# A two-layer attention and expert kernel: the low part of one norm chunk moves from VectorE to GpSimd, with a new order of calls in the first block

## The chip, the core and the metric

The kernel runs on one core of one Trainium2 chip. Its time is the device time of one execution in microseconds; the figure given is the median of several. The engines are TensorE (PE in the profile, its weight loads PEld), VectorE (DVE), ScalarE (ACT), GpSimd (POOL) and SyncE (SP), which here only issues transfers. Each runs its own list of instructions in order and waits on semaphores that the others raise.

## What is computed

The input x is 2 sequences of 1024 rows of 256 values, all float32. Cut to what matters:

```
x  = norm(x + x + softmax(causal(q k^T / 16)) v o_proj)       # q, k, v from norm(x)*gamma+beta, one head of width 256
h  = x + attention16(norm(x)*ln1_w+ln1_b)                     # 16 heads of width 128, rotary positions, causal
x  = norm(x + h + experts(norm(h)*ln2_w+ln2_b))               # 4 experts of width 256, the best 2 of each row mixed
```

(norm has no weights unless they are written behind it; the residual of each layer is added twice, since the layer adds it too.)

## The kernel before

**Split products.** TensorE multiplies in a rounded float32 form. To keep the precision, each operand x is held as a high part (x rounded, written by ScalarE) and a low part (x minus the high part, written by VectorE or GpSimd), and `product` (L438) issues three products: high by high, high by low and low by high. So nearly every tile goes PSUM, then ScalarE for the high part, then VectorE or GpSimd for the low part, and only then TensorE uses it.

**Units.** The attention work is 34 units: unit 0 and 1 are the two sequences in the first layer, units 2 to 33 the 16 heads of the second layer for both. A unit has the calls `project_q` (x = 0 to 3: query and key parts of the two 512-column chunks), `project_v` (4 groups), `scores(u, i)` for the eight 128-row tiles, the row maximum on VectorE (`row_max`), the exponent on ScalarE (`exponent`), `transposes(u, i)` of the probabilities into ps_t, their high part (`high_p`) and low part (`low_p`), and the product with the values (`first_outputs` in units 0 and 1, `outputs` and `out_project` later), which VectorE adds to `acc` (`accumulate`).

**The norms.** For a chunk c of 512 rows of a norm job: `ln_stats` (VectorE: statistics, L1576 to L1588), `ln_power` (GpSimd: the power -0.5, L2181), `ln_apply` (VectorE: four tensor_scalar on 128x256, L1636, or L1626 where x1 is written in place) or `ln_rows` (ScalarE), `ln_transpose` (TensorE, L487), `ln_affine` (ScalarE: weight and bias, once to `hf` in full and once rounded to `hT_hi`), and the low part hT_lo = hf - hT_hi. That last step is done by GpSimd in `ln_low` (L2207) for jobs 1 and up, and for job 0, chunk 1, by VectorE in `split_first` (L1643). Chunk 0 of job 0 is done in two halves by functions of its own (`half_stats`, `half_apply`, `half_transpose`, `half_affine`, `half_split`).

**What sets the order.** Nothing is scheduled at run time. For each engine the function `start` lists the calls of the first block by hand, up to unit 3; then `head(u)` repeats one fixed order for units 3 to 30, and `ends` lists the rest. The first block takes the first 140 us or so of the trace. Buffers are few: ps_m has two banks handed out in turn (`take_bank`, L414: a call waits until the user two before it has been emptied), ps_t has two banks, the rows of a norm chunk one buffer `rows`, and `hf` one. During the start TensorE also multiplies zeros (`warm`, L448), which are calls without use for the result.

Of the kernel before, what the change touches and what calls it, by code (L numbers as in the profile page):

```python
# [7 lines left out]
F32 = mybir.dt.float32  # L8
# [14 lines left out]
CH = 512  # L23
# [81 lines left out]
def build(nc, A):  # L105

    with ExitStack() as ctx:
# [6 lines left out]
        def event(name, order, step=1):  # L114
            return Event(sem(name), list(order), step)
# [94 lines left out]
        later = [key for key in ln_tiles if key[0] >= 1]  # L210
# [38 lines left out]
        hT_lo_dve = event("hT_lo_dve", ln_tiles[:4])  # L249
# [82 lines left out]
        def hT_event(job):  # L332
            return hT_lo_dve if job == 0 else hT_lo_pool
# [77 lines left out]
        def _(pe):  # L411
# [78 lines left out]
            def await_hT(job, c):  # L490
                ready = hT_event(job)
                pe.wait_ge(ready.sem, ready.at(job, c, KD - 1))
# [18 lines left out]
            def project_q(u, x):  # L511
# [181 lines left out]
            def start():  # L693
# [5 lines left out]
                warm(3)  # L699
                half_transpose(0)  # L700
                warm(4)
# [21 lines left out]
                transposes(0, 3)  # L723
                scores(0, 5)
                first_outputs(0, 0, 0)
# [11 lines left out]
                first_outputs(0, 1, 0)  # L737
                project_v(1, 0)
                project_q(1, 2)
                scores(1, 0)  # L740
                scores(1, 1)
                scores(1, 2)
                transposes(0, 7)
                project_q(1, 3)
                first_outputs(0, 1, 1)
                transposes(1, 0)
                scores(1, 3)
                transposes(1, 1)
                project_v(1, 1)
                project_v(1, 2)  # L750
                scores(1, 4)
                first_outputs(1, 0, 0)
                transposes(1, 2)
                transposes(1, 3)
# [15 lines left out]
                first_outputs(1, 1, 0)  # L770
                scores(2, 0)
                transposes(1, 7)
                scores(2, 1)
                project_q(2, 3)
                project_v(2, 2)
                scores(2, 2)
                transposes(2, 0)
                scores(2, 3)
                first_outputs(1, 1, 1)
                project_q(3, 0)  # L780
                transposes(2, 1)
                transposes(2, 2)
                scores(2, 4)
# [181 lines left out]
        def _(act):  # L965
# [36 lines left out]
            def ln_affine(job, c):  # L1002
                m, b = LN_VECTORS[job], job % 2
                for k in range(KD):
                    act.wait_ge(ln_mm.sem, ln_mm.at(job, c, k))
                    n = ln_f.place[job, c, k] - KD
                    if n >= 0:
                        before = ln_tiles[n]
                        ready = hT_event(before[0])
# [4 lines left out]
                    if not job:  # L1014
                        act.activation(hT_hi[:, b, k, c * CH:(c + 1) * CH], src, ACT.Identity, bias=ln_b[:, m, k:k + 1],
                                       scale=ln_w[:, m, k:k + 1])
# [163 lines left out]
            def start():  # L1180
# [16 lines left out]
                high_p(0, 1)  # L1197
                high_first(0, 3)
                exponent(0, 3)
                high_p(0, 2)  # L1200
                high_qk_weights(0, 0)
                high_values(0, 2)
                high_p(0, 3)
                high_values(0, 3)
                exponent(0, 4)
                double(0, 1)
                exponent(0, 5)
                high_p(0, 4)
                ln_affine(1, 0)
                double(1, 0)  # L1210
# [3 lines left out]
                high_first(1, 0)  # L1214
                high_p(0, 6)
                exponent(0, 7)
                high_first(1, 1)
                high_first(1, 2)
                high_values(1, 0)
                exponent(1, 0)  # L1220
                high_p(0, 7)
                high_first(1, 3)
                ln_rows(2, 0)
                exponent(1, 1)
                exponent(1, 2)
                high_p(1, 0)
                high_p(1, 1)
                high_values(1, 1)
                exponent(1, 3)
                high_values(1, 2)  # L1230
                exponent(1, 4)
                high_p(1, 2)
                high_p(1, 3)
                ln_affine(2, 0)
                ln_rows(2, 1)
                high_o_weights(0, 0)
                exponent(1, 5)
                high_values(1, 3)
                add_bias(2, 0)
                high_v_weights(0)  # L1240
                high_p(1, 4)
                ln_affine(2, 1)
                add_bias(2, 1)
                add_bias(2, 2)
                exponent(1, 6)
# [4 lines left out]
                high_values(2, 1)  # L1250
                high_p(1, 6)
                exponent(1, 7)
                high_qk_weights(0, 1)
                double(1, 1)
                high_p(1, 7)
                exponent(2, 0)
                add_bias(2, 3)
                high_p(2, 0)
# [3 lines left out]
                high_qk(2, 3)  # L1262
                exponent(2, 1)
                exponent(2, 2)
                add_bias(3, 0)
                exponent(2, 3)
                high_p(2, 1)
                high_p(2, 2)
                high_values(2, 3)
# [3 lines left out]
                high_qk(3, 0)  # L1273
# [3 lines left out]
                ln_affine(3, 0)  # L1277
                ln_rows(3, 1)
# [11 lines left out]
                exponent(3, 1)  # L1290
                high_qk(3, 2)
                high_qk(3, 3)
                high_o_weights(0, 1)
                exponent(3, 2)
                high_values(3, 1)
# [210 lines left out]
        def _(dve):  # L1506
# [1158 lines left out]
```

## Time and profile before

| | |
|---|---|
| median of 3 executions | 1120.58 us (1119.83 to 1121.37) |
| the profiled execution, its own time | 1120.56 us |
| its span, first to last instruction | 1118.7 us |
| TensorE busy | 1108.5 us, 99% |
| VectorE, ScalarE, GpSimd busy | 74%, 66%, 57% |
| mean granted TensorE clock | 0.997 |

The span leaves out 1.86 us of the profiled execution's time. Busy shares are those of the whole span; what an engine waited for is in the rows on waits. In a timeline row the duration of a TensorE instruction overlaps the next one, so the pace is read from one start to the next; a float32 product (transposes, `warm`) is recorded as two entries where the records are complete.

### The profile page before, as it was taken

To read this page: it belongs to the slowest core of one execution; us is meant where nothing else is said; L and a number is where in the kernel's file an instruction comes from. 1 tells how busy PE (TensorE), PEld (TensorE's weight loads), DVE (VectorE), ACT (ScalarE), POOL (GpSimd) and SP (SyncE) were. 2 spreads that over 40 slices of the span, in tenths; PEclk is the share of its full clock that TensorE was granted. 3 is DMA by queue.
4 is the path that set the end of the run, shared out by engine and by line. 5 is a ranking of instruction groups with operands and counts; after the bars stand their busy time and mean duration, and the time that the engine had idled before them with its cause. 6 is when DMAs were issued, how large, how long until landed. Compare 5 with 4: busy or idle time off the path is not lost.

```text
span 1118.7 us, 20425 instructions
## 1 busy us (share of the span) xinstructions
PE 1108.5 (99%) x7132; PEld 1012.9 (91%) x7132; DVE 830.4 (74%) x1978; ACT 743.3 (66%) x1577; POOL 640.1 (57%) x515
## 2 busy tenths in 40 slices
PE   9999999999999999999999999999999999999997
PEld 8999899999999999999999999999999999888996
DVE  7776777777777777777777777777777777875677
ACT  5666857666666666666666666666666666767664
POOL 2217666565556555565555555565555555867665
PEclk9999999999999999999999999999999999999999
DMA  4002412121212121212121212121212112221001
GB/s 176 1 1 62 128 39 53 39 62 39 52 40 62 38 53 38 63 38 53 38 62 39 52 39 62 39 51 38 59 37 52 38 44 57 58 85 58 1 20 57
DMA packets 33286, 56.55 MB, mean 51 GB/s; under 512 B 5792, under 2 KB 10016, under 8 KB 33184
## 3 DMA queue, kind: packets, MB, share of 16 engines
q1 hardware_dynamic: 33040, 55.21, 19.4%
q8 instruction: 58, 0.95, 0.4%
q14 instruction: 44, 0.36, 0.1%
q10 hardware_dynamic: 144, 0.03, 0.0%
HBM read 17.47 MB, written 4.19 MB: 19 GB/s over the span
## 4 chain that ended last, share of the span: by engine, by line
PE 95%; DVE 2%; issue 1%; DMA 1%; POOL 0%; ACT 0%; SPq 0%; POOLq 0%; DVEq 0%; ACTq 0%
PE ps_m L440 58%; PE ps_s L440 24%; PE ps_t L590 12%; PE ps_m L487 1%; DVE acc L1741 0%; PE ps_m L648 0%; DMA work<-in_attn_w 0%; DVE ps_s L1701 0%; PE ps_m L461 0%; DVE pT_lo L1708 0%; DVE rows L1636 0%; POOL qk_lo L2283 0%; PE ps_t L440 0%; DMA work<-work 0%; ACT work L1083 0%
## 5 line engine op out<-in xcount | busy, mean ns | idle before, releaser
L2225 POOL TENSOR_TENSOR work<-work,rope 128x512 f32<-128x512 f32 x128 | 166.9, 1304 | 224.4 <-DMA work<-work 224.3
L1708 DVE TENSOR_TENSOR pT_lo<-ps_t,pT_hi 128x512 fp32r<-128x512 f32 (+3 forms) x408 | 210.5, 550 | 27.9 <-ACT pT_hi L1132 25.7
L1132 ACT ACTIVATE pT_hi<-ps_t 128x512 fp32r<-128x512 f32 (+3 forms) x408 | 182.7, 489 | 70.1 <-PE ps_t L590 69.9
L1701 DVE CUSTOM_DVE_ANT_0 ps_s<-ps_s,causal 128x128 f32<-128x128 f32 (+7 forms) x272 | 203.3, 765 | 6.6 <-PE ps_s L440 4.2
L2236 POOL TENSOR_TENSOR qk_lo<-work,qk_hi 128x512 fp32r<-128x512 f32 x128 | 162.9, 1292 | 19.8 <-ACT qk_hi L1089 19.8
L2229 POOL TENSOR_TENSOR work<-work 128x512 f32<-128x512 f32 x128 | 167.8, 1311 | 10.0
L1741 DVE SCALAR_TENSOR_TENSOR acc<-ps_m,rinv,acc 128x256 f32<-128x256 f32 x272 | 118.7, 478 | 65.4 <-PE ps_m L440 64.2
L1083 ACT ACTIVATE work<-ps_m,bqk 128x512 f32<-128x512 f32 x128 | 88.7, 693 | 114.0 <-PE ps_m L440 114.0
L1125 ACT ACTIVATE prob_b<-ps_s,nmax 128x640 f32<-128x640 f32 (+3 forms) x136 | 130.3, 958 | 19.5 <-DVE nmax L1701 16.5
L440 PE MATMUL ps_s<-qk_hi 128*128 128x384 f32 (+5 forms) x384 | 141.1, 367 | 0.0
L1662 DVE SCALAR_TENSOR_TENSOR work<-ps_m,bqk,rope 128x512 f32<-128x512 f32 x128 | 95.4, 746 | 53.0 <-ACT work L1083 52.6
L440 PE MATMUL ps_m<-pT_lo,v_hi 128*128 128x512 f32 (+3 forms) x384 | 132.5, 345 | 0.0
L440 PE MATMUL ps_m<-pT_hi,v_lo 128*128 128x512 f32 (+3 forms) x384 | 132.5, 345 | 0.0
L440 PE MATMUL ps_s<-qk_lo,qk_hi 128*128 128x384 f32 (+5 forms) x384 | 131.6, 343 | 0.0
L440 PE MATMUL ps_s<-qk_hi,qk_lo 128*128 128x384 f32 (+5 forms) x384 | 131.5, 342 | 0.0
L440 PE MATMUL ps_m<-pT_hi,v_hi 128*128 128x512 f32 (+3 forms) x384 | 130.3, 339 | 0.0
L590 PE MATMUL ps_t<-ident,prob_b 128*128 128x128 f32 x884 | 120.1, 274 | 0.1
L590 PEld LDWEIGHTS ps_t<-ident,prob_b 128*128 128x128 f32 x884 | 99.9, 141 | 9.2 <-issue 0.7
L1089 ACT ACTIVATE qk_hi<-work 128x512 fp32r<-128x512 f32 x128 | 79.1, 641 | 43.2 <-POOL work L2229 43.0
L440 PE MATMUL ps_m<-hT_hi,wqk_hi 128*128 128x512 f32 x256 | 103.8, 406 | 0.0
L440 PE MATMUL ps_m<-hT_hi,wqk_lo 128*128 128x512 f32 x256 | 100.8, 394 | 0.0
L440 PE MATMUL ps_m<-hT_lo,wqk_hi 128*128 128x512 f32 x256 | 100.6, 393 | 0.0
(215 smaller groups left out, 2819.8 us busy)
## 6 DMA issues: line engine op xcount, KB each, us to landing
work<-work SPq DMA_DIRECT2D x256, 128.0 KB, 2.3
wst<-in_head_qk SPq DMA_DIRECT2D x16, 256.0 KB, 2.9
acc<-in_x_tiles SPq DMA_DIRECT2D x8, 256.0 KB, 6.6
wo_st<-in_L_ffn_wo SPq DMA_DIRECT2D x16, 128.0 KB, 2.3
wst<-in_pair_v SPq DMA_DIRECT2D x8, 256.0 KB, 3.0
x_rows<-acc SPq DMA_DIRECT2D x4, 512.0 KB, 3.6
wst<-in_expert SPq DMA_DIRECT2D x8, 256.0 KB, 2.8
rope<-x_rows SPq DMA_DIRECT2D x4, 512.0 KB, 3.6
```

The costliest lines, as they stand in the source:

```text
L440: ins = pe.matmul(out, lhs[x], rhs[y], start=first and k == 0, stop=last and k == 2)
L590: last = pe.transpose(t_bank(u, i, j)[:, k * P:(k + 1) * P], probs(i)[:, part], ident[:, :])
L1083: act.activation(qb[:, x % 2, :], m_bank("q", u, x), ACT.Identity, bias=bqk[:, j, head_:head_ + 1]).then_inc(qb_done.sem, qb_done.up(u, x))
L1125: act.activation(probs(i), all_scores[:, score_range(i)], ACT.Exp, bias=nmax[:, u % 2, i:i + 1], scale=-1.0, accum_out=rsum[:, u % 2, i:i ...
L1132: act.activation(pT_hi[:, slots, cols], t_bank(u, i, j)[:, 0:size * P].rearrange("p (j q) -> p j q", q=P), ACT.Copy).then_inc(t_hi.sem, t_ ...
L1662: dve.scalar_tensor_tensor(qc[:, ring3(u, x), :], m_bank("q", u, x), bqk[:, j, head_:head_ + 1], cos_t[:, c * CH:(c + 1) * CH], ALU.add, A ...
L1701: dve.tensor_tensor_reduce(s, s, causal[:, T - (i + 1) * P:T], -1.0, ABOVE_ALL, ALU.add, ALU.min, accum_out=nmax[:, u % 2, i:i + 1]).then_ ...
L1708: dve.tensor_tensor(pT_lo[:, slots, cols], t_bank(u, i, j)[:, 0:size * P].rearrange("p (j q) -> p j q", q=P), pT_hi[:, slots, cols].bitcas ...
L1741: last = dve.scalar_tensor_tensor(acc[:, b, tile, :], src[:, t * D:(t + 1) * D], rinv[:, u % 2, tile:tile + 1], acc[:, b, tile, :], ALU.mu ...
L2225: pool.tensor_tensor(qs[:, x % 2, :], qs[:, x % 2, :], sin_t[:, c * CH:(c + 1) * CH], ALU.mult).then_inc(sin_done.sem, sin_done.up(u, x))
L2229: pool.tensor_tensor(qc[:, ring3(u, x), :], qc[:, ring3(u, x), :], qs[:, x % 2, :], ALU.add).then_inc(rope_done.sem, rope_done.up(u, x))
L2236: pool.tensor_tensor(qk_lo[:, u % 2, j, cols], qc[:, ring3(u, x), :], qk_hi[:, u % 2, j, cols].bitcast(F32), ALU.subtract).then_inc(qk_lo_ ...
```

## The change

1. `split_first` goes. The low part of job 0, chunk 1 is made by GpSimd's `ln_low(0, 1)`, between `ln_power(0, 1)` and `ln_power(1, 0)`. It needs the high part's own event (ScalarE now raises `hT_hi_act` for it) and `ln_f`; TensorE and ScalarE wait on `hT_lo_pool` for this chunk.
2. The calls of `start` get a new order on all five engines. On TensorE `warm(4)` goes ahead of `half_transpose(0)`; `transposes(0, 0)` and `(0, 1)` go ahead of `project_q(0, 2)`; some thirty calls up to `scores(2, 4)` change places with a neighbour. On VectorE `half_apply(0)` goes ahead of `half_stats(1)`, and statistics, `ln_apply`, low parts and row maxima move by a few places each. On ScalarE the `double` calls (acc times 2, L972) come later, `ln_affine(0, 1)` comes ahead of `high_values(0, 1)`. On SyncE the weight loads and the spills `keep_x1` move among the `swap` transfers.

`head` and `ends` are as before. The core of the diff:

```diff
-        later = [key for key in ln_tiles if key[0] >= 1]
+        later = [key for key in ln_tiles if key[:2] != (0, 0)]
...
-        hT_lo_dve = event("hT_lo_dve", ln_tiles[:4])
+        hT_lo_dve = event("hT_lo_dve", ln_tiles[:2])
...
-        def hT_event(job):
-            return hT_lo_dve if job == 0 else hT_lo_pool
+        def hT_event(job, c):
+            return hT_lo_pool if job or c else hT_lo_dve
...
                     for k in range(KD):
-                        if x % 2 == 0 and not u:
-                            pe.wait_ge(hT_lo_dve.sem, hT_lo_dve.at(0, c, k))
+                        if not u:
+                            pe.wait_ge(hT_lo_pool.sem, hT_lo_pool.at(0, c, k))
...
-            def split_first(c):
-                cols = slice(c * CH, (c + 1) * CH)
-                for k in range(KD):
-                    dve.wait_ge(ln_f.sem, ln_f.at(0, c, k))
-                    dve.tensor_tensor(hT_lo[:, 0, k, cols], hf[:, k, :], hT_hi[:, 0, k, cols].bitcast(F32),
-                                      ALU.subtract).then_inc(hT_lo_dve.sem, hT_lo_dve.up(0, c, k))
-
...
                 for k in range(KD):
                     pool.wait_ge(hT_hi_act.sem, hT_hi_act.at(job, c, k))
+                    if not job:
+                        pool.wait_ge(ln_f.sem, ln_f.at(job, c, k))
...
                 scores(0, 3)
-                project_q(0, 2)
                 transposes(0, 0)
                 transposes(0, 1)
+                project_q(0, 2)
+                transposes(0, 2)
                 project_q(0, 3)
                 project_v(0, 2)
-                transposes(0, 2)
+                transposes(0, 3)
...
                 high_values(0, 0)
-                high_values(0, 1)
                 ln_affine(0, 1)
-                double(0, 0)
                 exponent(0, 0)
                 exponent(0, 1)
-                high_first(0, 2)
-                exponent(0, 2)
+                high_values(0, 1)
...
                 accumulate(0, 0, 1)
+                ln_apply(1, 1)
                 low_p(0, 4)
-                ln_apply(1, 1)
-                ln_stats(2, 0)
                 row_max(0, 6)
...
+                low_values(2, 1)
+                invert(1, 1)
                 low_p(1, 6)
-                low_values(2, 1)
-                row_max(2, 0)
-                invert(1, 1)
                 accumulate(1, 1, 0)
...
                 rotate(3, 1)
+                ln_apply(3, 1)
                 low_o(2, 0)
-                ln_apply(3, 1)
...
                 ln_power(0, 1)
+                ln_low(0, 1)
                 ln_power(1, 0)
                 ln_power(1, 1)
                 ln_low(1, 0)
+                ln_low(1, 1)
                 ln_power(2, 0)
-                ln_low(1, 1)
```

How the instructions stand, at four places. First TensorE at the very start, in the difference of the two orders: L446 is `warm`, L461 `fold_product`, L471 `half_transpose`.

```order
 L446 MATMUL ps_t<-prob_b 128x128 x10
 L461 MATMUL ps_m<-work 128x256 x4
-L446 MATMUL ps_t<-prob_b 128x128 x3
+L446 MATMUL ps_t<-prob_b 128x128 x4
 L471 MATMUL ps_s<-ident,rows 128x128 x4
-L446 MATMUL ps_t<-prob_b 128x128 x2
+L446 MATMUL ps_t<-prob_b 128x128
 L471 MATMUL ps_s<-ident,rows 128x128 x4
 L461 MATMUL ps_m<-work 128x256 x4
```

One of the products of zeros moves ahead of the first half's transposes; the second half's stand where they stood.

GpSimd from its first powers on, before (L2190 and L2181 are powers, L2207 is `ln_low`):

```order
L2190 TENSOR_TENSOR rstd<-var,minus_half 128x2 x2
L2181 TENSOR_TENSOR rstd<-var,minus_half 128x4 x3
L2207 TENSOR_TENSOR hT_lo<-hf,hT_hi 128x512 x2
L2181 TENSOR_TENSOR rstd<-var,minus_half 128x8
L2207 TENSOR_TENSOR hT_lo<-hf,hT_hi 128x512 x2
```

and after, where the same functions have the lines L2182, L2173 and L2201:

```order
L2182 TENSOR_TENSOR rstd<-var,minus_half 128x2 x2
L2173 TENSOR_TENSOR rstd<-var,minus_half 128x4
L2201 TENSOR_TENSOR hT_lo<-hf,hT_hi 128x512 x2
L2173 TENSOR_TENSOR rstd<-var,minus_half 128x4 x2
L2201 TENSOR_TENSOR hT_lo<-hf,hT_hi 128x512 x4
```

Two 128x512 subtractions are added between the first and the second chunk power, and the four of job 1 now stand together.

VectorE around `low_p(0, 4)`, before (L1741 is `accumulate(0, 0, 1)`, L1708 `low_p`, L1636 `ln_apply(1, 1)`, L1576 `ln_stats(2, 0)`):

```order
L1741 SCALAR_TENSOR_TENSOR acc<-ps_m,rinv,acc 128x256 x2
L1708 TENSOR_TENSOR pT_lo<-ps_t,pT_hi 128x4x128
L1708 TENSOR_TENSOR pT_lo<-ps_t,pT_hi 128x128
L1636 TENSOR_SCALAR rows<-acc,mv,rstd 128x256 x4
L1576 BN_STATS stats<-acc 128x6 x4
```

and after (L1734 `accumulate`, L1701 `low_p`, L1694 `row_max(0, 6)`):

```order
L1734 SCALAR_TENSOR_TENSOR acc<-ps_m,rinv,acc 128x256 x2
L1636 TENSOR_SCALAR rows<-acc,mv,rstd 128x256 x4
L1701 TENSOR_TENSOR pT_lo<-ps_t,pT_hi 128x4x128
L1701 TENSOR_TENSOR pT_lo<-ps_t,pT_hi 128x128
L1694 ISA ps_s,nmax<-ps_s,causal 128x896
```

The four instructions of `ln_apply(1, 1)` now stand ahead of the low parts that TensorE's `transposes(0, 5)` waits for.

VectorE near the end of the block, before (L1662 is `rotate(3, 1)`, L1714 `low_o(2, 0)`, L1626 `ln_apply(3, 1)`):

```order
L1662 SCALAR_TENSOR_TENSOR work<-ps_m,bqk,rope 128x512
L1714 TENSOR_TENSOR oT_lo<-ps_m,oT_hi 128x512
L1626 TENSOR_SCALAR acc<-acc,mv,rstd 128x256 x4
L1701 ISA ps_s,nmax<-ps_s,causal 128x896
L1701 ISA nmax 128x1
```

and after (L1655 `rotate`, L1707 `low_o`, L1694 `row_max`):

```order
L1655 SCALAR_TENSOR_TENSOR work<-ps_m,bqk,rope 128x512
L1626 TENSOR_SCALAR acc<-acc,mv,rstd 128x256 x4
L1707 TENSOR_TENSOR oT_lo<-ps_m,oT_hi 128x512
L1694 ISA ps_s,nmax<-ps_s,causal 128x896
L1694 ISA nmax 128x1
```

Here too `ln_apply` has passed a low part, that of the first head's output.

## Rows read from the trace of the kernel before

**Rows 1.** The page, part 1: busy time of each engine.

```profile
PE 1108.5 (99%) x7132; PEld 1012.9 (91%) x7132; DVE 830.4 (74%) x1978; ACT 743.3 (66%) x1577; POOL 640.1 (57%) x515
```

**Rows 2.** TensorE's waits, whole span: us in total, times, longest.

```profile
PE ps_t L446 <- POOL prob_b L2157: 1.0, 1, 1.0
PE ps_m L487 <- DVE oT_lo L1714: 0.5, 1, 0.5
PE ps_m L461 <- DMA work<-in_attn_w: 0.4, 1, 0.4
```

**Rows 3.** Busy time by stretch; last columns: clock, DMA share, GB/s.

```profile
0.00:140.00 140.00, 138.12 (x939) 128.26 (x940) 103.04 (x287) 94.34 (x191) 59.41 (x60) 1.00 0.23 74
...
140.00:270.00 130.00, 130.00 (x827) 118.65 (x826) 97.14 (x216) 84.47 (x186) 73.72 (x60) 1.00 0.20 47
```

**Rows 4.** Timeline of TensorE, the first 23 us: start, duration, instruction.

```profile
7.96 0.83 PE L446 MATMUL ps_t<-prob_b 128*128 128x128 f32 x6
8.63 0.60 PE L471 MATMUL ps_s<-ident,rows 128*128 128x128 f32 x4
...
20.56 0.34 PE L440 MATMUL ps_s<-hT_lo,qk_hi 128*128 128x384 f32 x1
20.74 0.34 PE L440 MATMUL ps_s<-hT_hi,qk_lo 128*128 128x384 f32 x1
21.06 0.50 PE L440 MATMUL ps_s<-hT_hi,qk_hi 128*128 128x512 f32 x1
...
22.56 0.45 PE L440 MATMUL ps_m<-hT_hi,wo_hi 128*128 128x512 f32 x1
...
23.99 0.49 PE L590 MATMUL ps_t<-ident,prob_s 128*128 128x128 f32 x3
```

**Rows 5.** Timeline of TensorE, three later places.

```profile
38.52 0.45 PE L440 MATMUL ps_s<-hT_hi,qk_hi 128*128 128x448 f32 x1
...
41.03 0.81 PE L590 MATMUL ps_t<-ident,prob_b 128*128 128x128 f32 x6
...
121.84 0.65 PE L487 MATMUL ps_m<-ident,rows 128*128 128x128 f32 x4 [0.48 <-DVE oT_lo L1714]
```

**Rows 6.** Timeline of ScalarE.

```profile
17.73 0.60 ACT L1094 ACTIVATE v_hi<-ps_m 128x512 fp32r<-128x512 f32 x1 [0.84 <-PE ps_m L440]
...
20.23 0.78 ACT L1017 ACTIVATE hf<-ps_s,vec 128x512 f32<-128x512 f32 x1
...
98.62 1.13 ACT L1125 ACTIVATE prob_b<-ps_s,nmax 128x1024 f32<-128x1024 f32 x1
```

**Rows 7.** Timeline of VectorE.

```profile
21.72 1.28 DVE L1643 TENSOR_TENSOR hT_lo<-hf,hT_hi 128x512 fp32r<-128x512 f32 x2
...
31.69 1.37 DVE L1636 TENSOR_SCALAR rows<-acc,mv,rstd 128x256 f32<-128x256 f32 x4
...
38.31 0.89 DVE L1708 TENSOR_TENSOR pT_lo<-ps_t,pT_hi 128x512 fp32r<-128x512 f32 x2 [0.25 <-ACT pT_hi L1132]
39.12 2.36 DVE L1636 TENSOR_SCALAR rows<-acc,mv,rstd 128x256 f32<-128x256 f32 x4
...
98.40 1.16 DVE L1708 TENSOR_TENSOR pT_lo<-ps_t,pT_hi 128x512 fp32r<-128x512 f32 x2 [1.53 <-ACT pT_hi L1132]
...
121.09 0.69 DVE L1714 TENSOR_TENSOR oT_lo<-ps_m,oT_hi 128x512 fp32r<-128x512 f32 x1 [1.31 <-ACT oT_hi L1141]
```

**Rows 8.** Timeline of GpSimd.

```profile
39.86 2.75 POOL L2207 TENSOR_TENSOR hT_lo<-hf,hT_hi 128x512 fp32r<-128x512 f32 x2 [9.40 <-ACT hT_hi L1020]
```

**Rows 9.** Busy time and clock (0.51) in one late stretch.

```profile
986.00:989.40 3.40, 3.40 (x13) 3.01 (x12) 2.11 (x7) 3.34 (x7) 3.32 (x3) 0.51 0.00 0
```

**Rows 10.** Timeline of TensorE in the stretch of the slow clock.

```profile
983.15 1.88 PE L648 MATMUL ps_m<-w_gate,hf 128*128 128x4 f32 x16
...
986.49 0.67 PE L440 MATMUL ps_s<-qk_hi 128*128 128x384 f32 x1
...
989.30 0.43 PE L440 MATMUL ps_m<-pT_lo,v_hi 128*128 128x512 f32 x1
```

More of the change, by code:

```diff
@@ L490, in await_hT @@
             def await_hT(job, c):
-                ready = hT_event(job)
+                ready = hT_event(job, c)
                 pe.wait_ge(ready.sem, ready.at(job, c, KD - 1))
@@ L770, in start @@
                 first_outputs(1, 1, 0)
+                transposes(1, 7)
+                project_q(2, 3)
                 scores(2, 0)
-                transposes(1, 7)
+                project_v(2, 2)
                 scores(2, 1)
-                project_q(2, 3)
-                project_v(2, 2)
+                transposes(2, 0)
                 scores(2, 2)
-                transposes(2, 0)
+                first_outputs(1, 1, 1)
                 scores(2, 3)
-                first_outputs(1, 1, 1)
                 project_q(3, 0)
+                scores(2, 4)
                 transposes(2, 1)
                 transposes(2, 2)
-                scores(2, 4)
                 project_v(2, 3)
@@ L1008, in ln_affine @@
                         before = ln_tiles[n]
-                        ready = hT_event(before[0])
+                        ready = hT_event(*before[:2])
                         act.wait_ge(ready.sem, ready.at(*before))
@@ L1205, in start @@
                 exponent(0, 4)
+                exponent(0, 5)
                 double(0, 1)
-                exponent(0, 5)
                 high_p(0, 4)
                 ln_affine(1, 0)
-                double(1, 0)
                 ln_affine(1, 1)
@@ L1214, in start @@
                 high_first(1, 0)
+                high_first(1, 1)
                 high_p(0, 6)
                 exponent(0, 7)
-                high_first(1, 1)
+                high_values(1, 0)
                 high_first(1, 2)
-                high_values(1, 0)
+                high_p(0, 7)
                 exponent(1, 0)
-                high_p(0, 7)
+                double(1, 0)
                 high_first(1, 3)
+                high_p(1, 0)
+                exponent(1, 1)
                 ln_rows(2, 0)
-                exponent(1, 1)
+                high_o_weights(0, 0)
                 exponent(1, 2)
-                high_p(1, 0)
+                high_values(1, 1)
                 high_p(1, 1)
-                high_values(1, 1)
                 exponent(1, 3)
                 high_values(1, 2)
-                exponent(1, 4)
                 high_p(1, 2)
@@ L1248, in start @@
                 high_qk(2, 0)
-                high_qk(2, 1)
[L1250 to L1254, printed above, removed]
+                double(1, 1)
+                high_p(1, 6)
+                high_qk_weights(0, 1)
+                high_values(2, 1)
+                exponent(1, 7)
+                high_qk(2, 1)
                 high_p(1, 7)
+                add_bias(2, 3)
                 exponent(2, 0)
-                add_bias(2, 3)
-                high_p(2, 0)
                 high_qk(2, 2)
@@ L1289, in start @@
                 exponent(3, 0)
-                exponent(3, 1)
+                high_values(3, 1)
                 high_qk(3, 2)
                 high_qk(3, 3)
-                high_o_weights(0, 1)
+                exponent(3, 1)
                 exponent(3, 2)
-                high_values(3, 1)
                 exponent(3, 3)
@@ L1831, in start @@
                 half_stats(0)
+                half_apply(0)
                 half_stats(1)
-                half_apply(0)
                 half_apply(1)
@@ L1923, in start @@
                 row_max(2, 2)
+                low_values(2, 2)
+                low_p(2, 0)
                 low_qk_weights(0, 1)
+                accumulate(1, 1, 1)
                 row_max(2, 3)
-                low_p(2, 0)
-                low_values(2, 2)
-                accumulate(1, 1, 1)
                 ln_stats(3, 1)
@@ L1932, in start @@
                 rotate(3, 0)
+                low_values(2, 3)
                 low_p(2, 2)
-                low_values(2, 3)
                 low_p(2, 3)
                 row_max(2, 5)
+                invert(2, 0)
                 rotate(3, 1)
+                ln_apply(3, 1)
                 low_o(2, 0)
-                ln_apply(3, 1)
                 row_max(2, 6)
-                invert(2, 0)
                 accumulate(2, 0, 0)
```

139 lines of the change are left out of this document (72 added, 67 removed).

## The prediction

> **What bounds the kernel now.** I read the page's busy shares first, then TensorE's waits, then busy time by stretch, and last the timelines of the first block. The first view settles most of it: TensorE is busy for 1108.5 of 1118.7 us, and the next engine, VectorE, for 830.4 [rows 1]. So only two things can change the time: what TensorE has to multiply, and how long it stands. The change adds no product and takes none away; it only puts them in another order. Work that goes from VectorE to GpSimd counts only where TensorE stood for it.
>
> How much can be won is read from the stretches. In the first 140 us, where every moved call lies, TensorE is busy for 138.12 us; in the next 130 us, where the fixed order runs, for all 130.00 [rows 3]. So the block's idle time is 1.88 us. Three waits make it up [rows 2]: 1.0 us before the first product of zeros, for GpSimd's first memset; 0.4 us for the first weights from memory; and 0.48 us at 121.84, where an `ln_transpose` waits until VectorE has emptied a bank (the low part of the output, L1714) [rows 5]. No moved call touches the first two. Small stalls hide in the pace of starts: a 384-column product takes 0.18 us to the next start (20.56 to 20.74), but the one at 20.74 takes 0.32 us, since the next, the first of `scores(0, 3)`, waits for ScalarE's `hf` (20.23 plus 0.78 is 21.01) [rows 4, 6]. That is a stall of 0.14 us, and a few of this size are all that is left beside the 0.48 us.
>
> **The change, part by part.** The sum is made against the profiled execution, 1120.56 us (span 1118.7 and 1.86 around it), which is 0.02 us under the median of 1120.58.
>
> *The low part itself.* VectorE loses two 128x512 subtractions, 1.28 us [rows 7]. GpSimd gets them, at 2.75 us for two when VectorE works beside it [rows 8]. The inputs are there when ScalarE has written `hf` the second time, at 21.01 [rows 6]. The second subtraction then ends at about 21.01 plus 1.38 (half of 2.75), 22.4. In the new order TensorE ends `scores(0, 3)` at 22.56, does the three products of `transposes(0, 0)` and `(0, 1)` (at most 0.49 us by their recorded duration [rows 4]), and starts `project_q(0, 2)` no earlier than about 22.8; the second low part is wanted after its first three products. Six products of `scores(0, 3)` took 21.06 to 22.56, 0.25 us each [rows 4], so that is about 23.5. Slack 1.1 us: cost 0. The cover is `scores(0, 3)` itself, 1.5 us; without it TensorE would stand for 0.4 us. The saved 1.28 us of VectorE are worth 0 too, because VectorE was not what TensorE waited for here. Behind the new work on GpSimd stands `ln_power(1, 0)`, whose result VectorE wants for `ln_apply(1, 0)`, at 31.69 before [rows 7]; a delay to about 24 is harmless.
>
> *The start.* One product of zeros now precedes the first half's transposes. Three of them took 7.96 to 8.63, so one is 0.22 us [rows 4]. The transposes of half 0 come 0.22 us later, and ScalarE with them; those of half 1 do not move. `half_apply(0)` goes ahead of `half_stats(1)`, which costs VectorE nothing since it waits for the input there. What can reach TensorE is ScalarE's delay, through the fold's low part and the rows of chunk 1. Ends: 0 and +0.22. I take +0.1, as ScalarE's own chain has gaps that take up part.
>
> *`ln_affine(0, 1)` ahead of `high_values(0, 1)`.* ScalarE starts that value part at 17.73, pace 0.5 us [rows 6], before the norm's chunk. Now the norm's chunk goes first and can start when the transposes end, which is hardly earlier. Ends: 0 and the whole stall of 0.14 us. I take -0.05.
>
> *`ln_apply(1, 1)` ahead of `low_p(0, 4)`.* Before, `low_p(0, 4)` ran at 38.31 for 0.89 us and `ln_apply` at 39.12 for 2.36 us [rows 7]. Now `ln_apply` starts when the transposes of chunk (1, 0) have read `rows`, at about 38.6, just after `scores(0, 6)` starts at 38.52 [rows 5]. At 1.37 us, as at 31.69 [rows 7], it ends at 40.0, and `low_p(0, 4)` at 40.9. TensorE wants it at 41.03 for `transposes(0, 5)` [rows 5]. Slack 0.1 us. At 2.36 us, the duration that the same instructions had while GpSimd worked from 39.86 [rows 7, 8], `low_p` would end at 41.9 and TensorE would stand for 0.9 us. So the ends are 0 and +0.9. I take 0, since three of the four instructions are over before 39.86.
>
> *`low_p(1, 6)` behind `low_values(2, 1)` and `invert(1, 1)`.* It ran at 98.40, 0.2 us before `exponent(1, 7)` started at 98.62 for 1.13 us [rows 7, 6]; `invert(1, 1)` wants that exponent, so `low_p(1, 6)` can start only at about 99.8 if ScalarE keeps its time, and at about 99.2 if ScalarE, which now skips a wait for the turned query part, comes 0.6 us earlier. It ends 1.2 us later, and `transposes(1, 7)`, now just ahead of `project_q(2, 3)`, wants its first half at about 99.9. Ends: 0 and +0.9. I take +0.1, near the low end, since ScalarE's wait goes.
>
> *`ln_apply(3, 1)` ahead of `low_o(2, 0)`.* VectorE stood 1.31 us for ScalarE before `low_o` at 121.09 [rows 7]; `ln_apply` at 1.37 us nearly fits in. TensorE's wait at 121.84 follows `low_o` directly [rows 5]. Ends: 0 where it fits, +1.05 where it is slowed to 2.36 (1.31 of it covered). I take 0: GpSimd's next job there waits for a transfer.
>
> The rest of the moves (SyncE's weight loads and spills, `double`, row maxima, GpSimd's turns) leave each buffer ready before TensorE comes, by my count of the new order; ends -0.48 (the wait at 121.84 gone) and +0.3, value 0.
>
> A rule that speaks against the change: the rows show `ln_apply` at 2.36 us beside GpSimd and at 1.37 us without it [rows 7, 8]. The Trainium skill says this too (SBUF — State Buffer, section Who interferes with whom): VectorE and GpSimd share one pair of ports, and it is held for a whole instruction, so a tensor_scalar in a two-port mode and a GpSimd operation shut each other out. The trace agrees in direction, with 0.99 us for four instructions. By that rule the 2.7 us of new GpSimd work at 19.5 to 22.4 would slow VectorE only if an `ln_apply` or a cast ran there; row maxima, statistics and value parts stand there, with one operand from SBUF, so it adds nothing.
>
> **Sum.** +0.1 - 0.05 + 0 + 0.1 + 0 = +0.15; 1120.56 + 0.15 = 1120.7 us. In words: no change that can be measured.
>
> **The rivals.**
>
> *The new order takes the block's waits away.* For it: the wait of 0.48 us and the stall of 0.14 us that hides in the pace. Against it: the bank wait at 121.84 hangs on the end of `outputs(2, 0)`, ScalarE's high part and VectorE's low part, in this order before and after. It would give 1120.56 - 0.48 - 0.14 = 1119.9 us, a gain under 0.1%.
>
> *Slower: `ln_apply` now delays low parts.* One mechanism at two places, 38.6 and 119.8: the four tensor_scalar run beside GpSimd at 2.36 us, and the low part behind them is what TensorE waits for. Price 0.9 + 1.05, with the +0.22 of the start and 0.1 at `transposes(1, 7)`: 1120.56 + 2.27 = 1122.8 us. It decides as soon as GpSimd's subtraction starts before the second of the four. For it: the slacks are 0.1 us. Against it: at both places GpSimd is idle or comes late by my count.
>
> *TensorE's clock.* From 986.0 to 989.4 the granted clock is 0.51, the lower level of 1.2 GHz, and TensorE had just done 16 gate products of 4 columns, from 983.15, and waited twice [rows 9, 10]. Products start at half pace: from 986.49 to 989.30 it got through three of 384 columns and four of 512, which take 3 x 0.18 and 4 x 0.25 us at full clock [rows 4, 10], so 2.81 - 1.54, some 1.3 us, are lost. The change shifts this stretch by tenths of a microsecond and leaves its content as it was. Should the drop not come, the time is 1120.7 - 1.3 = 1119.4 us; a second drop would cost as much.
>
> **How the numbers follow.** Forecast 0.74, with a range of its own of 1120.0 to 1121.5. Waits gone 0.10. Clock 0.06. Slower through `ln_apply` 0.10. Two medians of this kernel can be told apart from about 0.2% on, 2.2 us: below 1118.3 or above 1122.8. Faster needs the waits and the clock together: 0.03. Slower needs nearly all of the second rival: two thirds of its 0.10, and a little for stalls that I overlooked, 0.08. Within: 0.89. The range for 8 in 10 takes in the two gains and most of the slow case: 1119.2 to 1122.3.
>
> **What would show it.** In the trace after: TensorE's busy time in the first 140 us within 0.7 us of 138.12; `project_q(0, 2)` starting without a wait on GpSimd, at about 22.8; L1636's third group at 38.6 with a duration near 1.4 us; the wait of the later `ln_transpose` still there, near 0.5 us; the fixed order beginning within 0.5 us of its old place. The forecast falls if a wait on L2201 (GpSimd's low part) stands in TensorE's list, if `low_p` ends after TensorE's `transposes(0, 5)` or `(1, 7)` could start, or if the next 130 us are no longer full.

## The result, and the profile after

The changed kernel takes 1122.08 us in the median of 14 executions (1120.69 to 1124.49), the kernel before 1120.82 (1119.24 to 1121.37, 14 executions beside it). The ratio is 1.0016, with a 95% interval of 1.0009 to 1.0024: a cost of some 1.8 us, between 1.0 and 2.7. The two medians by themselves are 1.26 us apart. The forecast was 1120.7 us in a range of 1119.2 to 1122.3, and no change that can be measured; the time lies in the range, the change is there.

The two profiled executions hide this. That of after took 1120.87 us with a span of 1119.1, only 0.4 us above the span of before. The cause is TensorE's clock: the profile of before contains the 3.4 us at the lower clock [rows 9], that of after does not. So compare where the fixed order starts, at the first product of `project_q(4, 0)`, and subtract where `project_half` starts, since the first weights land at a different time in each execution. The rows of after, TensorE's timeline (start, duration, instruction):

```profile
11.55 0.47 PE L440 MATMUL ps_t<-hT_hi,wo_hi 128*128 128x256 f32 x1
...
145.75 0.40 PE L440 MATMUL ps_m<-hT_hi,wqk_hi 128*128 128x512 f32 x1
```

And of before:

```profile
11.60 0.47 PE L440 MATMUL ps_t<-hT_hi,wo_hi 128*128 128x256 f32 x1
...
144.10 0.40 PE L440 MATMUL ps_m<-hT_hi,wqk_hi 128*128 128x512 f32 x1
```

The distance, called the **length of the first block** below, is 134.20 us after and 132.50 before: +1.70 us, inside the interval of the ratio and free of the clock. In the 130 us that follow, TensorE is busy throughout in both. Busy time by stretch of after, beside [rows 3, 9] (the last but two columns are clock, DMA share and GB/s):

```profile
0.00:140.00 140.00, 136.65 (x931) 126.90 (x932) 102.78 (x285) 92.56 (x186) 60.51 (x61) 1.00 0.23 74
140.00:270.00 130.00, 130.00 (x824) 118.58 (x823) 95.58 (x214) 85.67 (x191) 73.33 (x58) 1.00 0.19 46
986.00:989.40 3.40, 3.06 (x22) 2.62 (x22) 3.40 (x12) 1.59 (x3) 3.32 (x4) 1.00 0.00 0
```

TensorE lost 138.12 - 136.65 = 1.47 us in the first 140. Its waits after (beside [rows 2]) name two new ones:

```profile
PE ps_t L446 <- POOL prob_b L2149: 1.0, 1, 1.0
PE ps_t L590 <- DVE pT_lo L1701: 0.9, 1, 0.9
PE ps_m L487 <- DVE oT_lo L1707: 0.6, 1, 0.6
...
PE ps_s L440 <- POOL qk_lo L2230: 0.4, 1, 0.4
PE ps_m L461 <- DMA work<-in_attn_w: 0.4, 1, 0.4
```

**First place, `transposes(0, 5)`.** VectorE, GpSimd and TensorE after, in this order (beside [rows 5, 7, 8]):

```profile
38.79 2.43 DVE L1636 TENSOR_SCALAR rows<-acc,mv,rstd 128x256 f32<-128x256 f32 x4 [0.82 <-PE ps_m L487]
41.14 0.88 DVE L1701 TENSOR_TENSOR pT_lo<-ps_t,pT_hi 128x512 fp32r<-128x512 f32 x2
...
39.77 2.60 POOL L2201 TENSOR_TENSOR hT_lo<-hf,hT_hi 128x512 fp32r<-128x512 f32 x2 [6.36 <-ACT hT_hi L1020]
...
40.74 0.37 PE L440 MATMUL ps_s<-hT_hi,qk_lo 128*128 128x448 f32 x1
41.96 0.85 PE L590 MATMUL ps_t<-ident,prob_b 128*128 128x128 f32 x6 [0.86 <-DVE pT_lo L1701]
```

`ln_apply(1, 1)` took 2.43 us instead of 1.37. The durations of its four instructions (shortest, median and longest in ns, then the first and last start), after and before:

```profile
L1636 DVE TENSOR_SCALAR rows<-acc,mv,rstd x4: 411/412/1456, 38.8 to 39.8; 128x256 f32<-128x256 f32 x4
...
L1636 DVE TENSOR_SCALAR rows<-acc,mv,rstd x4: 403/408/1391, 39.1 to 40.1; 128x256 f32<-128x256 f32 x4
```

Only one of the four is long, in both. After, the first three start 0.33 us apart; the fourth starts at 39.8, GpSimd had started at 39.77, and the fourth takes 1.46 us instead of 0.41. TensorE's next start came 1.22 us behind one of pace 0.20: 1.02 us lost.

**Second place, `scores(2, 4)`.** TensorE, GpSimd and SyncE's queue after:

```profile
113.23 0.39 PE L440 MATMUL ps_m<-hT_hi,wqk_lo 128*128 128x512 f32 x1
114.06 0.38 PE L440 MATMUL ps_s<-qk_hi 128*128 128x320 f32 x1 [0.44 <-POOL qk_lo L2230]
...
108.29 1.31 POOL L2219 TENSOR_TENSOR work<-work,rope 128x512 f32<-128x512 f32 x1 [1.90 <-DMA work<-work]
109.68 1.29 POOL L2223 TENSOR_TENSOR work<-work 128x512 f32<-128x512 f32 x1
110.93 2.99 POOL L2230 TENSOR_TENSOR qk_lo<-work,qk_hi 128x512 fp32r<-128x512 f32 x2
...
104.67 0.60 SPq L2474 DMA_DIRECT2D work<-work  x1
105.31 0.58 SPq L2482 DMA_DIRECT2D x_rows<-acc  x1
```

The same places before:

```profile
105.96 1.29 POOL L2236 TENSOR_TENSOR qk_lo<-work,qk_hi 128x512 fp32r<-128x512 f32 x1 [4.11 <-ACT qk_hi L1089]
107.28 1.42 POOL L2225 TENSOR_TENSOR work<-work,rope 128x512 f32<-128x512 f32 x1
...
111.14 1.30 POOL L2236 TENSOR_TENSOR qk_lo<-work,qk_hi 128x512 fp32r<-128x512 f32 x1 [0.74 <-ACT qk_hi L1089]
...
112.37 0.71 PE L590 MATMUL ps_t<-ident,prob_s 128*128 128x128 f32 x5
112.83 0.39 PE L440 MATMUL ps_s<-qk_hi 128*128 128x320 f32 x1
```

Here the start comes 0.83 us behind one of pace 0.23: 0.60 us lost. Three edits meet: on GpSimd `low_qk(2, 2)` went behind `turn(2, 3)`, so both low parts now stand at the end (110.93, ending at 113.9); on TensorE `scores(2, 4)` went ahead of five products of 128 columns; on SyncE a spill of 512 KB (L2482) went right behind the `swap` that `turn(2, 3)` waits for. What each is worth is the matter of f1 to f3 and g2. 1.02 + 0.60 and 0.1 at the `ln_transpose` make the 1.7 us.

### The profile page after: what moved, and what is told of

Same layout as the page of the kernel before. It is cut to its first block, busy times and chain, and to the rows that moved or that the text cites. A ratio compares the mean times of both kernels' runs of the same rounds, so it can differ in the third digit from the quotient of the medians.

```text
span 1119.1 us, 20428 instructions
## 1 busy us (share of the span) xinstructions
PE 1107.3 (99%) x7132; PEld 1011.5 (90%) x7132; DVE 830.2 (74%) x1976; ACT 743.2 (66%) x1577; POOL 642.4 (57%) x517
## 4 chain that ended last, share of the span: by engine, by line
PE 93%; DVE 2%; POOL 2%; issue 1%; ACT 1%; DMA 0%; POOLq 0%; SPq 0%; DVEq 0%; ACTq 0%
PE ps_m L440 56%; PE ps_s L440 23%; PE ps_t L590 11%; PE ps_m L487 1%; DVE rows L1636 1%; POOL work L2219 0%; DVE acc L1734 0%; POOL work L2223 0%; PE ps_m L648 0%; DMA work<-in_attn_w 0%; DVE pT_lo L1701 0%; DVE ps_s L1694 0%; PE ps_m L461 0%; POOL qk_lo L2230 0%; POOL qk_lo L2277 0%
## 5 line engine op out<-in xcount | busy, mean ns | idle before, releaser
L1701 DVE TENSOR_TENSOR pT_lo<-ps_t,pT_hi 128x512 fp32r<-128x512 f32 (+3 forms) x408 | 210.7, 551 | 28.5 <-ACT pT_hi L1132 26.0
L1694 DVE CUSTOM_DVE_ANT_0 ps_s<-ps_s,causal 128x128 f32<-128x128 f32 (+7 forms) x272 | 203.5, 767 | 6.5 <-PE ps_s L440 4.2
L1734 DVE SCALAR_TENSOR_TENSOR acc<-ps_m,rinv,acc 128x256 f32<-128x256 f32 x272 | 118.8, 478 | 63.6 <-PE ps_m L440 63.4
L1655 DVE SCALAR_TENSOR_TENSOR work<-ps_m,bqk,rope 128x512 f32<-128x512 f32 x128 | 95.5, 746 | 49.6 <-ACT work L1083 49.3
```

The costliest lines, as they stand in the source:

```text
L1655: dve.scalar_tensor_tensor(qc[:, ring3(u, x), :], m_bank("q", u, x), bqk[:, j, head_:head_ + 1], cos_t[:, c * CH:(c + 1) * CH], ALU.add, A ...
L1694: dve.tensor_tensor_reduce(s, s, causal[:, T - (i + 1) * P:T], -1.0, ABOVE_ALL, ALU.add, ALU.min, accum_out=nmax[:, u % 2, i:i + 1]).then_ ...
L1701: dve.tensor_tensor(pT_lo[:, slots, cols], t_bank(u, i, j)[:, 0:size * P].rearrange("p (j q) -> p j q", q=P), pT_hi[:, slots, cols].bitcas ...
L1734: last = dve.scalar_tensor_tensor(acc[:, b, tile, :], src[:, t * D:(t + 1) * D], rinv[:, u % 2, tile:tile + 1], acc[:, b, tile, :], ALU.mu ...
```

## The experiments

The kernels ran in three groups of four, each group with executions of before on its chip. "Block" is the length of the first block in the profiled execution; before has 132.50, after 134.20. In brackets behind a ratio stands its 95% interval. By these intervals only e3, g3 and g4 are clearly apart from before; smaller differences are read from the blocks, of one trace each. How far such a length can be trusted: g3 and g4 have the same calls up to its end, and differ by 0.25 us.

**e1_lowp_first**, on after:

```diff
-                ln_apply(1, 1)
                 low_p(0, 4)
+                ln_apply(1, 1)
```

> The changed kernel with one pair of VectorE calls back in the old order: low_p(0, 4) ahead of ln_apply(1, 1). Landmark in every expectation: the start of the first product of project_q(4, 0), in the fixed order, at 144.10 us in the trace before and 145.75 us in the trace after. Theory A (the loss is made at single waits of TensorE, the largest of them 0.86 us at transposes(0, 5), because VectorE's last ln_apply instruction is shut out by a GpSimd instruction): TensorE's wait at transposes(0, 5) goes, landmark 1.0 us earlier, about 144.8; time 1.0 us under the changed kernel, some 0.3 to 0.7 us over the kernel before. Rival B (the added GpSimd work slows the block as a whole, by contention with VectorE): landmark stays within 0.3 us of 145.75, the wait turns up elsewhere.

Ratio to before 1.0008 [0.9999, 1.0018], 1120.18 us beside 1119.28. Block 133.74. The wait at `transposes(0, 5)` is gone, although `ln_apply` still takes 2.35 us; but the wait at `scores(2, 4)` grew:

```profile
40.13 0.89 DVE L1701 TENSOR_TENSOR pT_lo<-ps_t,pT_hi 128x512 fp32r<-128x512 f32 x2 [0.25 <-ACT pT_hi L1132]
40.93 2.35 DVE L1636 TENSOR_SCALAR rows<-acc,mv,rstd 128x256 f32<-128x256 f32 x4
...
115.42 0.38 PE L440 MATMUL ps_s<-qk_hi 128*128 128x320 f32 x1 [0.76 <-POOL qk_lo L2230]
```

**e2_gpsimd_waits**, on after; GpSimd's `ln_low(1, 0)` may start only when `ln_apply(1, 1)` is done:

```diff
                 ln_power(1, 1)
+                pool.wait_ge(rows_dve.sem, rows_dve.at(1, 1, TC - 1))
                 ln_low(1, 0)
```

> The changed kernel, order untouched, but GpSimd's ln_low(1, 0) waits until ln_apply(1, 1) is over. Theory A: the four instructions take about 1.37 us instead of 2.43, from 38.8; low_p(0, 4) ends near 41.0; TensorE's wait at transposes(0, 5) is 0.2 us or nothing; landmark 0.9 to 1.0 us earlier. If the loss were the order itself (low parts behind four more instructions), and not the shutting out, the wait stays near 0.86 us. GpSimd's low parts of chunk (1, 0) start at about 40.15 instead of 39.77 and nobody waits for that.

Ratio 1.0006 [0.9997, 1.0015], 1120.02 us beside 1119.28. Block 133.37. The order on VectorE is that of after, only the overlap is gone, and `ln_apply` takes 1.38 us again:

```profile
40.85 1.38 DVE L1636 TENSOR_SCALAR rows<-acc,mv,rstd 128x256 f32<-128x256 f32 x4 [0.82 <-PE ps_m L487]
42.15 0.88 DVE L1701 TENSOR_TENSOR pT_lo<-ps_t,pT_hi 128x512 fp32r<-128x512 f32 x2
...
42.31 2.52 POOL L2201 TENSOR_TENSOR hT_lo<-hf,hT_hi 128x512 fp32r<-128x512 f32 x2 [6.85 <-DVE rows L1636]
```

`low_p` beside GpSimd from 42.31 keeps its 0.88 us. One of its operands is in PSUM, where `ln_apply` reads and writes SBUF alone; no run tests whether that is the reason.

**e3_before_apply_first**, on before, the opposite edit of e1 (`ln_apply(1, 1)` ahead of `low_p(0, 4)`).

> The kernel before with one pair of VectorE calls in the new order: ln_apply(1, 1) ahead of low_p(0, 4), nothing else. Theory A: the same 2.4 us for ln_apply, a wait of 0.9 us at transposes(0, 5), landmark from 144.10 to about 145.1, time 1.0 us over before (ratio 1.0009). Rival B: no change, below 0.3 us.

Ratio 1.0011 [1.0001, 1.0020]. Block 133.50: this one exchange costs 1.0 us.

```profile
38.92 2.43 DVE L1636 TENSOR_SCALAR rows<-acc,mv,rstd 128x256 f32<-128x256 f32 x4 [0.82 <-PE ps_m L487]
...
42.09 0.84 PE L590 MATMUL ps_t<-ident,prob_b 128*128 128x128 f32 x6 [0.86 <-DVE pT_lo L1708]
```

**e4_before_low_gpsimd**, on before: only part 1 of the change (the low part of chunk 1 by `ln_low(0, 1)`).

> The kernel before with the low part of chunk 1 of the first norm made by GpSimd and no other call moved (VectorE's split_first is left out, GpSimd's ln_low(0, 1) put behind ln_power(0, 1)). My step in the prediction: GpSimd's second low part ends at 22.4, TensorE wants it at about 23.3, cost 0; VectorE's 1.28 us are worth nothing; landmark within 0.15 us of 144.10, time within 0.2 us of before. Rival B: landmark and time later by 0.5 us or more. Rival C (freeing VectorE is worth something by itself and the new order threw it away): landmark earlier by 0.3 us or more.

Ratio 1.0005 [0.9996, 1.0015]. Block 132.40: the part that gave the change its name neither costs nor gains anything in the first block.

**f1_qk_order**, e1's edit and on GpSimd:

```diff
-                turn(2, 3)
                 low_qk(2, 2)
+                turn(2, 3)
                 low_qk(2, 3)
```

> The kernel after with two edits: low_p(0, 4) ahead of ln_apply(1, 1) on VectorE (as in e1_lowp_first), and on GpSimd low_qk(2, 2) back ahead of turn(2, 3), where it stood before the change. Theory A (GpSimd's own order makes scores(2, 4) wait): in e1_lowp_first GpSimd stood 2.44 us for the swap transfer while low_qk(2, 2), 1.29 us, was ready; put there, it leaves the chain turn(2, 3), low_qk(2, 3) shorter by one subtraction of 1.3 to 1.5 us, so the wait of 0.8 us on qk_lo goes altogether, and the fixed order starts 0.9 us earlier than in e1_lowp_first, counted from project_half, at about 132.8; time 1119.3 to 1119.8 us beside a before of 1119.3, ratio 1.000 to 1.0005. Theory B (the transfer comes late because the spill shares the DMA engines, the order does not matter): the turn still ends at 112.3, the last low part 1.3 to 1.5 us later; the wait shrinks by the same amount, so this run alone does not refute B; B says the 2.44 us wait for the transfer only changes its place and is still about 1.2 us behind the subtraction. Theory C (TensorE comes too early since scores(2, 4) was moved ahead of two transposes): the wait is set by GpSimd's end, and it goes here too, but only by the 1.3 us that GpSimd gains.

1119.83 us beside 1120.34, ratio 0.9997 [0.9988, 1.0006]. Block 132.52, before's length. No wait on `qk_lo` is left; `low_qk(2, 2)` fills the time of the transfer:

```profile
106.09 1.29 POOL L2230 TENSOR_TENSOR qk_lo<-work,qk_hi 128x512 fp32r<-128x512 f32 x1 [0.74 <-ACT qk_hi L1089]
107.34 1.49 POOL L2219 TENSOR_TENSOR work<-work,rope 128x512 f32<-128x512 f32 x1
...
110.94 1.29 POOL L2230 TENSOR_TENSOR qk_lo<-work,qk_hi 128x512 fp32r<-128x512 f32 x1 [0.74 <-ACT qk_hi L1089]
```

**f2_spill_back**, e1's edit and `keep_x1(0, 0)` back behind `swap(3, 0)` on SyncE.

> As e1_lowp_first, and on SyncE the spill keep_x1(0, 0) (512 KB) moved back behind load_qk_weights(1, 0) and swap(3, 0). Theory B (the spill slows the swap): swap(2, 3) lands after about 2.3 to 2.6 us instead of 4.1 us after its second issue, GpSimd's turn(2, 3) starts 1.3 to 1.6 us earlier than in e1_lowp_first, and the wait at scores(2, 4), 0.93 us in the pace, is gone; fixed order at about 132.8 from project_half. Theory A: the transfer lands as late as in e1_lowp_first and the wait stays near 0.9. Theory C, as A.

Ratio 1.0008 [0.9999, 1.0017]. Block 133.18. The spill is not what makes the transfer late: without it the turn starts 3.63 us after the second issue, in after, with it, 108.29 - 104.67 = 3.62:

```profile
103.81 0.60 SPq L2474 DMA_DIRECT2D work<-work  x1
...
107.44 1.30 POOL L2219 TENSOR_TENSOR work<-work,rope 128x512 f32<-128x512 f32 x1 [1.90 <-DMA work<-work]
```

Across executions with the spill this time varies by itself: 3.6 us in after, 3.8 in e2, 4.1 in e1, where the blocks of e2 and e1 are 0.37 us apart. But late it is. The same 128 KB, from the second issue to their landing (last number, us), in g2, in f2 and in after:

```profile
work<-work SPq DMA_DIRECT2D x1, 128.0 KB, 2.9
...
work<-work SPq DMA_DIRECT2D x1, 128.0 KB, 3.6
...
work<-work SPq DMA_DIRECT2D x1, 128.0 KB, 3.6
```

In the five traces with before's order of transfers (before, e3, e4, f4, g2) it is 2.8 to 3.0 us, in the nine with the new order (f2: all but the spill) 3.5 to 4.1. So something in SyncE's new order other than this spill makes the transfer some 0.6 us later, about as much as the whole second loss; what it is stays open, since no run puts that order back.

**f3_scores_back**, e1's edit and `scores(2, 4)` back behind `transposes(2, 1)` and `(2, 2)` on TensorE.

> As e1_lowp_first, and on TensorE scores(2, 4) back behind transposes(2, 1) and transposes(2, 2), as before the change. Theory C (the call came too early): the five or so products of 128 columns take about 0.7 us, so the excess of 0.93 us falls to 0.2 us or less, unless the transposes themselves wait for ScalarE's exponent; fixed order at about 133.0 from project_half. Theories A and B expect the same reduction, since all three add up in one slack; what this run tells is how much of the wait the order on TensorE alone carries. If the excess stays at 0.9, the transposes had their own wait there and the order on TensorE is innocent.

Ratio 1.0001 [0.9992, 1.0010]. Block 132.89. The stall falls from 0.93 us in e1 to 0.48 (the start of `scores(2, 4)` comes 0.94 us after that of the transposes, 0.46 before), less than expected: GpSimd's end sets it, and moving the call gives only the length of the transposes.

**g1_qk_only**, after with f1's GpSimd edit alone.

> The kernel after with one edit: on GpSimd low_qk(2, 2) back ahead of turn(2, 3). ln_apply(1, 1) stays ahead of low_p(0, 4). Theory (two separate losses): the stall of 1.0 us ahead of transposes(0, 5) stays, the wait on qk_lo at scores(2, 4) is gone; start of the fixed order, counted from project_half, at 133.5 (after 134.2, before 132.5). Rival (one loss, the second is only the echo of the first): with ln_apply(1, 1) left, scores(2, 4) still waits and the fixed order starts at 134.2.

Ratio 1.0009 [1.0000, 1.0018]. Block 133.61 (expected 133.5). The first stall stays whole, the second is gone: they are two losses.

```profile
PE ps_t L590 <- DVE pT_lo L1701: 0.8, 1, 0.8
```

**g2_before_qk**, on before: `low_qk(2, 2)` behind `turn(2, 3)`, nothing else.

> The kernel before with one edit: on GpSimd low_qk(2, 2) behind turn(2, 3) instead of ahead of it. Theory: the last low part ends at 112.9 to 113.3 instead of 112.44, while TensorE wants it from 113.1 on, where scores(2, 4) stands two transposes later than in after; a stall of 0.1 to 0.5 us, fixed order at 132.6 to 133.0 from project_half. Rival (the order on GpSimd costs nothing without TensorE's earlier scores(2, 4)): 132.5.

Ratio 1.0006 [0.9997, 1.0015], block 132.50: the rival holds. GpSimd's pair ends at 114.83, TensorE wants it at 114.99 and does not wait:

```profile
112.28 2.55 POOL L2236 TENSOR_TENSOR qk_lo<-work,qk_hi 128x512 fp32r<-128x512 f32 x2
...
114.99 0.39 PE L440 MATMUL ps_s<-qk_hi 128*128 128x320 f32 x1
```

So GpSimd's move alone costs nothing in the kernel before, with a slack of 0.16 us left. But f3 has the same two orders as g2 at this place, on GpSimd and on TensorE, and still a stall of 0.48. Counted from `project_half`, its pair of low parts ends 0.49 us later than that of g2: 0.25 because the turn starts later, and 0.24 because the turn and the pair take longer (the pair 3.00 us for 2.55). The second loss therefore has three parts: GpSimd's order, whose mending alone removes it (g1, f1); TensorE's call, worth 0.46; and a chain behind the transfer that is later and slower in the new order.

**f4_bank_and_ends**, on before, an attempt at something faster:

```diff
-                ln_transpose(3, 0)
                 scores(2, 6)
+                ln_transpose(3, 0)
...
+                scores(LAST, 2)
                 gate_logits(0, 0)
-                ln_transpose(4, 1)
-                scores(LAST, 2)
                 scores(LAST, 3)
+                ln_transpose(4, 1)
```

> The kernel before (not after) with two moves on TensorE: ln_transpose(3, 0) behind scores(2, 6), so that the bank that low_o(2, 0) empties is wanted 1.3 us later, and in the last block scores(LAST, 2) ahead of gate_logits(0, 0) and scores(LAST, 3) ahead of ln_transpose(4, 1), so that the 16 products of 4 columns and the transposes that wait for accumulate no longer stand next to each other. Theory: the wait of 0.48 us at 121.84 goes, and the 3.4 us at the lower clock, which cost some 1.3 us in the executions that have them, do not come; median 1118.9 to 1119.6 us where before has 1119.3 or 1120.8 according to how many of its runs have the low clock; ratio 0.9985 to 0.9996. Rival: the low clock is not set off by the neighbourhood of the gate products and comes all the same in some runs, then only the 0.5 us of the bank is won, ratio 0.9996; or scores(2, 6) waits for its own inputs, and nothing is won.

A miss: ratio 1.0009 [1.0000, 1.0018], 1121.05 us beside 1120.34, block 133.21. The scores had covered ScalarE's emptying of the transposes' banks. Now the next output product waits for it, in each of the two places:

```profile
PE ps_m L440 <- ACT hT_hi L1020: 2.2, 2, 1.1
```

**g3_two_fillers**, as f1, with `scores(2, 7)` behind that transpose and `transposes(2, 5)` ahead of `out_project(2, 0, 1)`.

> After with both losses mended (as f1_qk_order), and on TensorE scores(2, 6) ahead of ln_transpose(3, 0), scores(2, 7) behind it, out_project(2, 0, 0), transposes(2, 5), out_project(2, 0, 1). In f4_bank_and_ends the wait for low_o only changed into one of 1.1 us for ScalarE's ln_affine behind the transpose. Theory (a transpose of the norm needs a product of over 1 us on both sides): with scores(2, 7), 1.4 us, behind it and transposes(2, 5), 0.6 us, between the two output products both waits are gone; fixed order 0.5 us earlier than in f1_qk_order, at 132.0 from project_half, time 1119.0 to 1119.6 beside a before of 1119.3 to 1120.3, ratio 0.9990 to 0.9998. Rival: ScalarE's ln_affine comes 1.3 us later than before, and its delay shows at transposes(2, 6) or scores(3, 0), so the 0.5 us comes back; 132.5.

A miss again: ratio 1.0016 [1.0007, 1.0025], block 134.42. Both waits are gone, and a third stands there, since `low_p(2, 4)`, whose bank `transposes(2, 5)` needs, is behind `accumulate(2, 0, 0)` on VectorE, which waits for the output product (VectorE, then TensorE):

```profile
126.39 0.88 DVE L1734 SCALAR_TENSOR_TENSOR acc<-ps_m,rinv,acc 128x256 f32<-128x256 f32 x2 [1.90 <-PE ps_m L440]
127.19 0.88 DVE L1701 TENSOR_TENSOR pT_lo<-ps_t,pT_hi 128x512 fp32r<-128x512 f32 x2
...
128.02 0.85 PE L590 MATMUL ps_t<-ident,prob_b 128*128 128x128 f32 x6 [1.76 <-DVE pT_lo L1701]
```

**g4_fillers_and_end**, as g3, with `scores(LAST, 2)` ahead of `gate_logits(0, 0)`.

> As g3_two_fillers, and in the last block scores(LAST, 2) ahead of gate_logits(0, 0), with scores(LAST, 3) left behind ln_transpose(4, 1). Theory: the wait of 0.34 us for accumulate ahead of that transpose goes, a wait of about 0.6 us for ScalarE's ln_affine comes ahead of outputs(LAST - 1, 1), and the 3.4 us at the lower clock never come (f4_bank_and_ends had a mean clock of 0.998 or 0.999 in all 11 executions, its before 0.997 in 11 of 33). So against g3_two_fillers 0.3 us slower where that has no low clock, and 1.0 us faster where it has; median within 0.4 us of it. Rival: the low clock comes also here, then it is simply 0.3 us slower.

Ratio 1.0016 [1.0007, 1.0024], 1121.89 us beside g3's 1121.64; a wait of 0.40 us on ScalarE came at the expected place (0.6 was expected). (The 11 of 33 in the expectation is 10 on record.)

## Why the prediction was wrong

- **The low part itself, 0:** right. e4 has a block 0.1 us shorter than before. In after, GpSimd ran it at 19.88 for 2.62 us, no wait on it, and `project_q(0, 2)` began at 22.88 (predicted 22.8).
- **The start (+0.1) and `ln_affine(0, 1)` (-0.05):** near nothing in sum, as said; TensorE's start ahead of `scores(0, 3)` came 0.35 us behind one of pace 0.17 after, where 0.32 had stood. The length of the first block leaves out what stands ahead of `project_half`, so this term is seen only in part.
- **`ln_apply(1, 1)` ahead of `low_p(0, 4)`, taken at 0 in a range up to +0.9: this step failed.** It costs 1.02 us (e3: 1.00 alone). The place, the rows and the slack of 0.1 us were right; the size was not. The reason given, three of four instructions over before 39.86, was true and did not help: the one instruction left is held for nearly the whole subtraction, 2.43 - 1.38 = 1.05 us of its 1.28. The row of before said so already. There, with starts 0.33 us apart from 39.12, the third was running at 39.86 and only the fourth was still to come, and the four took 2.36 us all the same. So the slower rival's condition, that GpSimd starts before the second of the four, was too strict as well. e2 shows the mechanism by taking the overlap away. The Trainium skill says the same (SBUF — State Buffer, section Who interferes with whom): whoever issues first has the shared pair for its whole instruction and the other is blocked fully. The trace agrees, with one instruction of 1.46 us among three of 0.41. I had quoted that rule for the new work at 19.5 and not applied it here.
- **`low_p(1, 6)`, +0.1:** 0. The eight transposes of `transposes(1, 7)` took 0.82 us to the next start in both, and TensorE is busy without a gap from 95 to 105.
- **`ln_apply(3, 1)` ahead of `low_o(2, 0)`, 0:** right, 1.37 us as assumed; the wait at that `ln_transpose` went from 0.48 to 0.58.
- **The rest of the moves, 0 (-0.48 to +0.3): this step failed too,** by +0.60 at `scores(2, 4)`, twice my upper end. I had looked at the order of each engine by itself; the loss is in their sum (g2: 0 for GpSimd's move alone), with a transfer that lands in 3.6 us where it had landed in 3.0. It was the only term without a place and a row of its own.
- **The rivals.** The slower one had the right mechanism and the wrong second place: GpSimd's transfer did keep it away from `ln_apply(3, 1)`. Its price of 1122.8 was an upper end. The clock rival was real and outside the sum: it made the two profiled executions look alike. The sum's last figures also agree with the profile of after: 1120.56 + 1.7 - 1.3 for the missing stretch is 1121.0, and it took 1120.87.

With the two terms at their measured size the sum is 1120.56 + 1.02 + 0.60 + 0.1 = 1122.3 us; the median is 1122.08. The two losses add up: where the transfer is as late as in after, mending the first gives back 1.02 us (f2), the second alone 0.59 (g1), both 1.68 (f1). That e1 and e2 give back only 0.46 and 0.83 goes with a later transfer, 4.1 and 3.8 us to the turn's start for 3.6. As for the clock, 7 of the 14 executions of after have a mean of 0.997; that of the 14 of before is not on record, so what share of the difference between the medians is the clock's cannot be said.

## What to carry to other kernels

Price an overlap of VectorE and GpSimd on the ports that they share by the instruction of the other engine (here 1.05 us of 1.28), not by the share of time in common, and ask only whether one instruction starts inside it. Where an order is rewritten on several engines, check each wait against the moves of both sides together, since a move that is free alone (g2) can cost 0.6 us together with others. A transfer's waiting time on an in-order engine is the place for work that is ready; work moved from ahead of it to behind it comes that much later (f1 and g1 against e1 and after).

## What the runs showed of the hardware

The same hold shows in e4 for a single instruction: in before the scaling of a 128x256 tile at 19.91 took 0.35 us, beside GpSimd's new low part 1.35.

```profile
21.34 1.35 DVE L1685 TENSOR_SCALAR bv_sum<-wo_st,vec 128x256 f32<-128x256 f32 x1
...
21.24 2.64 POOL L2208 TENSOR_TENSOR hT_lo<-hf,hT_hi 128x512 fp32r<-128x512 f32 x2 [3.44 <-ACT hf L1017]
```

In after that call had moved to 71.2, which is why it did no harm there.

The 3.4 us at 1.2 GHz come in some executions of one and the same kernel. Of the fourteen profiled traces the three with a mean clock of 0.997 (before, e1, f2) have the stretch, and the eleven others do not. By that sign before had it in 16 of 97 executions, after in 7 of 14, and f4 and g4, the two kernels that change the order there, in none of 22. f4 has `scores(LAST, 3)` between the gate products and the transposes; g4 leaves them side by side and only takes away the wait of 0.34 us between them. That speaks for this place as the cause, but weakly: the share in before itself went from 1 of 31 to 10 of 33 from group to group, e2, e3 and e4, which change nothing there, have it in none of 30, and beside g4 before had it in 5 of 33. f4 also put a wait of 1.1 us there and g4 one of 0.4, so neither was faster. This stays open.
